# Carrying rows as fp16 halves out of attention: one DMA transpose for each x tile in place of TensorE transposes

## The reference

```python
h = tok(x)                                   # 768 -> 192, bias
h = layernorm(h + attn(h))                   # 12 heads of 16, tokens of one image
h = layernorm(h + ffn(h))
# ffn: y = expert(h, w1s, w2s, w3s)          (shared, width 768)
#      + sum over the best 2 of 8 experts of weight * expert(h, w1[e], w2[e], w3[e])
# expert(x) = (silu(min(x@W1, 10)) * clip(x@W3, -10, 10)) @ W2
# scores = sqrt(softplus(h @ gate_w)); choice by scores + gate_bias
```

## Time and profile before

| | us |
|---|---|
| median of 3 runs | 647.45 (644.85 to 650.32) |
| the profiled execution | 642.51 |
| its span, first to last instruction | 640.7 |
| PE busy | 540.3 |
| DVE busy | 455.9 |
| ACT busy | 357.5 |
| POOL busy | 182.8 |

### The profile page before, as it was taken

One profiled execution on the slowest core, in us unless ns is written; L12 is line 12 of the kernel. 1 busy time (PEld: TensorE's weight loads), 2 busy tenths in 40 slices (PEclk: granted clock), 3 DMA queues, 4 the chain that ended last, 5 costly groups with the idle time before them and its releaser, 6 DMA issues.

```text
span 640.7 us, 15246 instructions
## 1 busy us (share of the span) xinstructions
PE 540.3 (84%) x4208; PEld 410.0 (64%) x4209; DVE 455.9 (71%) x1064; ACT 357.5 (56%) x644; POOL 182.8 (29%) x210
## 2 busy tenths in 40 slices
PE   8899999899998668487739999999999999999451
PEld 7777878778787655275426666666666666667340
DVE  0376978878788766769836777777777777777385
ACT  1777696876968706544324555555555555555134
POOL 3102405224052221248750122221112222222422
PEclk9999999999999758989778999999999999999887
DMA  8334446364461513645534655555555555555833
GB/s 319 130 102 157 133 122 189 105 200 125 128 190 49 162 58 92 158 104 129 126 97 91 115 109 116 106 117 113 116 109 117 117 117 117 111 109 118 273 63 110
DMA packets 152890, 82.00 MB, mean 128 GB/s; under 512 B 120432, under 2 KB 148096, under 8 KB 151712
## 3 DMA queue, kind: packets, MB, share of 16 engines
q1 hardware_dynamic: 148144, 70.09, 45.1%
q0 software_dynamic: 4720, 11.60, 5.7%
HBM read 41.83 MB, written 15.83 MB: 90 GB/s over the span
## 4 chain that ended last, share of the span: by engine, by line
PE 64%; DVE 11%; POOL 8%; issue 8%; ACT 4%; DMA 4%; SPq 0%; ACTq 0%; DVEq 0%; POOLq 0%
PE bank L705 24%; PE bank L719 11%; PE bank L544 7%; POOL dbuf L1514 6%; DMA arena<-arena 3%; PE bank L622 3%; PE bank L571 3%; PE bank L583 3%; PE bank L693 3%; PE bank L634 3%; PE bank L559 3%; POOL rout L1477 1%; PE bank L637 1%; DVE arena L1015 1%; PE bank L742 1%
## 5 line engine op out<-in xcount | busy, mean ns | idle before, releaser
L705 PE MATMUL bank<-W,arena 128*128 (+1 forms) x1220 | 215.3, 333 | 2.1 <-DVE arena L1229 1.6
L705 PEld LDWEIGHTS bank<-W,arena 128*128 128x128 f16 x1220 | 120.5, 100 | 78.8 <-issue 7.7
L719 PE MATMUL bank<-W,arena 128*128 (+1 forms) x1098 | 102.7, 249 | 16.8 <-DVE arena L1238 16.8
L719 PEld LDWEIGHTS bank<-W,arena 128*128 128x128 f16 x1098 | 93.9, 99 | 25.7 <-issue 18.8
L1536 POOL DMA_INDIRECT ybuf<-arena,slot x43 | 41.9, 975 | 203.8 <-ACT arena L940 203.8
L1229 DVE TENSOR_SCALAR arena<-bank,sct 128x384 f32<-128x384 f32 x86 | 58.2, 677 | 39.9 <-PE bank L705 39.7
L924 ACT ACTIVATE arena<-bank,sct 128x384 f32<-128x384 f32 x86 | 49.9, 580 | 58.6 <-PE bank L705 58.5
L932 ACT ACTIVATE arena<-arena,sct 128x384 f16<-128x384 f32 x86 | 52.9, 615 | 46.3 <-DVE arena L1232 23.1
L1232 DVE SCALAR_TENSOR_TENSOR arena<-arena 128x384 f32<-128x384 f32 x122 | 68.3, 560 | 4.2
L1220 DVE SCALAR_TENSOR_TENSOR arena<-arena,sct 128x384 f16<-128x384 f32 x86 | 52.9, 615 | 15.8 <-ACT arena L932 15.7
L544 PE MATMUL bank<-arena,par 128*96 128x288 f32 x192 | 62.2, 416 | 0.5 <-ACT arena L832 0.5
(11 more groups left out here) (165 smaller groups left out, 836.6 us busy)
## 6 DMA issues: line engine op xcount, KB each, us to landing
arena<-xT SPq DMA_DIRECT2D x8, 864.0 KB, 4.7
stage<-w_all SPq DMA_DIRECT2D x9, 768.0 KB, 4.5
stage<-w_all SPq DMA_DIRECT2D x5, 1344.0 KB, 7.0
W<-w_all SPq DMA_DIRECT2D x4, 1344.0 KB, 7.1
arena<-dbuf SPq DMA_DIRECT2D x43, 96.0 KB, 2.0
dbuf<-arena SPq DMA_DIRECT2D x6, 679.0 KB, 9.1
W<-ybuf POOLq DMA_DIRECT2D x3, 1152.0 KB, 9.4
arena<-arena SPq DMA_TRANSPOSE x122
```

The costliest lines, as they stand in the source:

```text
L705: m = pe.matmul(bank[2 * k + n][:, 0:I // 2], xT16[:, b, lo, tail, :], W16[:, bass.ds(off + at + col, I // 2)], start=(z == 0), stop=(z == ...
L719: m = pe.matmul(bank[6][:, 0:C], hhT[b][:, ic // 3, lo, ic % 3, :], W16[:, bass.ds(off + at + ic * C, C)], start=(ic == 0 and z == 0), sto ...
```

## The change

A row is split once, in attention, and travels as fp16: 128 high values, 64 high values twice, 128 rest values, 64 rest values twice (HX = 512 numbers, 1024 bytes). A new DRAM buffer `xb16` holds these; `dbuf` rows grow from 194 to 264 fp32 words (the 512 halves, row number, weight, zeros). Each x tile is then one DMA transpose from `xb16` or `dbuf` straight into `xT16`: X, `x_hi`, `x_lo` and the three loads are gone (a load of 8 bytes a row stays for the routed steps). In attention POOL gets `split_rows(g)`, DVE `split_lo(g-1)`, SP `store_split(g-1)`. `hsp` has two buffers, so `h_hi(i)` waits for the transposes of step i-2 instead of i-1, and SP's `turn_h` stands after the x tile of two steps on (it was three). U(0) goes ahead of the last `proj`; the last `weights_lo_main` of attention goes behind `h_lo(0)`. COUNT_AT is 4, so the counts and choices are formed one step later. The core of the diff:

```diff
-HW = C + 2
+HX = 4 * C1
+DX = HX + 16
+HW = DX // 2
-            COUNT_AT = 3
+            COUNT_AT = 4
@@ SP, attention
+            def store_split(g):
+                sp.wait_ge(s_h16, g + 1)
+                sp.dma_start(xb16[bass.ds(g * GT, GT), :].rearrange("(t p) n -> p t n", p=TM),
+                             h16g).then_inc(s_x16o, 16)
@@ SP, group(g)
                 if choice:
                     zero_rows((g - 1) * ZPART, ZPART)
                     store_choice(g - 1)
+                if choice:
+                    store_split(g - 1)
                 if store:
                     store_group(g)
@@ POOL, attention
+            def split_rows(g):
+                wait_apart(pool, s_h1, g * GTILES + GTILES)
+                if not first(g):
+                    wait_apart(pool, s_x16o, g * 16)
+                PO.tensor_scalar(h16g[:, :, 0:C], h1g, XS, None, ALU.mult)
+                PO.tensor_scalar(h16g[:, :, C:2 * C1], h1g[:, :, C1:C], XS, None, ALU.mult).then_inc(s_h16h, 1)
...
                 if not last:
                     h0b_out(g + 1)
+                split_rows(g)
@@ DVE, attention
+            def split_lo(g):
+                wait_apart(dve, s_h16h, g + 1)
+                for at, a in ((2 * C1, 0), (2 * C1 + C, C1)):
+                    m = V.scalar_tensor_tensor(out=h16g[:, :, at:at + C - a], in0=h1g[:, :, a:C], scalar=XS,
+                                               in1=h16g[:, :, a:C], op0=ALU.mult, op1=ALU.subtract)
+                m.then_inc(s_h16, 1)
...
                 mask_max(g, 0)
                 weights_scale(g, wtotal)
+                if not start:
+                    split_lo(g - 1)
                 sums(g, 0)
                 mask_max(g, 1)
...
-                weights_lo_main(g, odd)
-                if last:
-                    x_lo(0, 0)
+                if not last:
+                    weights_lo_main(g, odd)
                 norm(g, between)
+                if last:
+                    split_lo(g)
                 between(ROUTE_G)
@@ SP, feed-forward
-            def load_x(row, b):
-                for at, a, n in ((0, 0, C1), (C1, C1, C2), (C, C1, C2)):
-                    sp.dma_start(xt[:, b, at:at + n], xbuf[bass.ds(row, XT), a:a + n]).then_inc(s_xl[b], 16)
+            def turn_x(n, b, rows):
+                if not (isinstance(n, int) and n < 2):
+                    wait_apart(sp, s_ud, n * 4 - 4)
+                sp.dma_start_transpose(xT16[:, b].rearrange("p z c n -> p (z c) n"), rows).then_inc(s_xl[b], 16)
...
                 def body(n, b):
-                    sp.wait_ge(s_xd, n - 1)
-                    load_x((n - skipped) * XT, b)
-                    turn_h(n - 3, 1 - b)
+                    turn_x(n, b, shared_rows(n - skipped))
+                    turn_h(n - 2, b)
@@ PE, feed-forward
             def U(i, b, off):
-                pe.wait_ge(s_xT, i + 1)
+                wait_apart(pe, s_xl[b], x_landed(i, b))
...
                 cur = cur(i)
-                if more:
-                    X(i + 1, 1 - b)
                 U(i, b, cur)
@@ ACT, feed-forward
-                    if not first(i):
-                        act.wait_ge(s_hT16[q], i * 16)
+                    if not (isinstance(i, int) and i < 2):
+                        act.wait_ge(s_hT16[b][q], (i - b) * 8)
```

More of the change, by code:

```diff
@@ L189, in over, with front @@
             return view(v.bitcast(F16) if dt == F16 else v, shape)
[L191 to L202, removed]
+        f_at = dict(zip([n for n, _ in F_SIZES], np.cumsum([0] + [n for _, n in F_SIZES]).tolist()))
+        def front(name, shape, dt=F32):
+            at = f_at[name]
+            v = arena[:, at:at + dict(F_SIZES)[name]]
+            return view(v.bitcast(F16) if dt == F16 else v, shape)
+        PSP = 1536
+        xT16 = front("xT16", (2, 2, 2, XT), F16)
+        sg, up = front("sg", (I,)), front("up", (I,))
+        hsp = [front("hsp0", (2, 2, I // 2), F16), view(par[:, PSP:PSP + I].bitcast(F16), (2, 2, I // 2))]
+        assert PSP + I <= PAR["wproj"][0]
+        yy = front("yy", (2, C))
+        hhT = [front(f"hhT{b}", (2, 2, IC // 2, XT), F16) for b in range(2)]
+        h16_raw = arena[:, H_FROM:H_FROM + SHT * HW]
+        h16 = view(h16_raw.bitcast(F16), (SHT, DX))
+        h16_id = view(h16_raw.bitcast(I32), (SHT, HW))[:, :, ROW_ID]
+        h16_w = view(h16_raw, (SHT, HW))[:, :, ROW_W]
+        h16_pad = view(h16_raw, (SHT, HW))[:, :, ROW_W + 1:HW]
+        h1 = acc = view(arena[:, H_FROM + SHT * HW:H_FROM + SHT * (HW + C)], (SHT, C))
+        assert H_FROM <= B_FROM
+        h16g = view(W16[0:TM, E * WF + 2 * (UPW + DNW):(E + 1) * WF], (GTILES, HX))
+        slot = view(slot_raw[:, :], (RTILES, 2))
         assert 2 * WF == SHT * 2 * C * 2
@@ L443, in _, with shared_rows @@
             group(GROUPS - 2, 0, load=False)
-            def load_x(row, b):
-                for at, a, n in ((0, 0, C1), (C1, C1, C2), (C, C1, C2)):
-                    sp.dma_start(xt[:, b, at:at + n], xbuf[bass.ds(row, XT), a:a + n]).then_inc(s_xl[b], 16)
[L450 to L473, removed]
+            def turn_x(n, b, rows):
+                if not (isinstance(n, int) and n < 2):
+                    wait_apart(sp, s_ud, n * 4 - 4)
+                sp.dma_start_transpose(xT16[:, b].rearrange("p z c n -> p (z c) n"), rows).then_inc(s_xl[b], 16)
+            def shared_rows(n):
+                return xb16[bass.ds(n * XT, XT), :]
             def turn_h(i, b):
@@ L517, in _ @@
             tiles_from(sp, SH2, ALLT, next_x(RTILES))
-            for i in range(ALLT - 3, ALLT):
+            for i in range(ALLT - 2, ALLT):
                 turn_h(i, i % 2)
@@ L772, in group @@
                 else:
[L773 to L774 removed]
+                    U(0, 0, 0)
                 proj(g)
@@ L796, in _ @@
             tiles_from(pe, SH2 + 2, ALLT - 1, lambda i, b: step(i, b, shared, shared))
-            step(ALLT - 1, (ALLT - 1) % 2, shared, shared, more=False)
+            step(ALLT - 1, (ALLT - 1) % 2, shared, shared)
             for i in (ALLT - 2, ALLT - 1):
@@ L949, in final_norm, with step @@
                 m.then_inc(s_fn, 1)
-            def step(i, b, cur, more=True):
-                if more:
-                    x_hi(i + 1, 1 - b)
+            def step(i, b, cur):
                 silu(i, scale(i, SILU_S) if cur else shc[:, SILU_S:SILU_S + 1])
-                h_hi(i, scale(i, H_S) if cur else shc[:, H_S:H_S + 1])
+                h_hi(i, b, scale(i, H_S) if cur else shc[:, H_S:H_S + 1])
             act.wait_ge(s_par, 32)
@@ L1241, in y_add, with step @@
                                        op0=ALU.mult, op1=ALU.add).then_inc(s_y, 1)
-            def step(i, b, cur, more=True, aside=None):
-                if more:
-                    x_lo(i + 1, 1 - b)
+            def step(i, b, cur, aside=None):
                 if aside:
@@ L1356, in _ @@
             up_h(0, *CLIPS)
-            x_lo(1, 1)
+            h_lo(0, 0, shc[:, H_S:H_S + 1])
+            weights_lo_main(GROUPS - 1, 1)
             steps = choice(GROUPS - 1)
@@ L1425, in _ @@
             for i in range(SH2, ALLT):
-                step(i, i % 2, False, more=(i < ALLT - 1))
+                step(i, i % 2, False)
                 if i > SH2 + 1:
```

154 lines of the change are left out of this document (83 added, 71 removed).

## The result

The kernel got slower. Against the kernel before, on one chip, the changed kernel takes 680.14 us (median of 4, 671.33 to 684.52) to 646.24 (median of 4). The forecast was 663 us, 639 to 681. On that chip the medians of the two kernels are 680.10 and 644.71.

The account below looks back on a forecast made before the run. PE was taken to set the pace in feed-forward, with DVE close beside it in attention. Attention +33.5, group 7 and start +8.5, first routed tile -3.5, steps 12 to 60 -18.5, end -4: +16 on 647.45, 663 us, range 639 to 681.

Parts of the forecast that it names:

- the first routed tile: From the last scatter to U(12): U(11) and D(9) done before, U(12) starting earlier but at the lower clock; -3.5 us.
- The wait: Attention: POOL's split waits for the previous group's store to land, holding DVE; 5.2 us a group after 1.42 us of slack.
- The clock: Attention: after idling, PE runs transposes and projections ahead of `heads` at the lower clock; 1.5 us a group (0 to 2.5).
- Steps 12 to 60: Routed steps: without X each step is 0.38 us shorter, the loop-end gap staying; -18.5 us.
- The sign that I had set down for being wrong: Profile signs against the forecast: landing under 4 us, POOL split under 1.2 us, or PE waiting for x tiles or h.
- rival (a): Routed steps: DMA transposes become the pace (SP or rings late), so the 18.5 us are not gained; +34, 682 us; 10%.
- Group 7 and start: Group 7's wait, U(0) ahead of `proj`, the added split and the later count, up to the first scatter; +8.5 us.
- The end: Last steps: two hsp buffers let h(58) split early, so D(57) follows the landing at once; -4 us.
- The point of decision: About 4.2 us a group in attention, above which attention costs more than feed-forward gives.
- rival (c): Attention: stores land before POOL asks, only DVE's hidden 1.15 us remain; -22, 625 us; 5%.

Follow-up runs that it names:

- e1: Changed kernel with SP issuing the store of the previous group's split rows ahead of its waits for the weights: 657.32 us, ratio 0.9805 to the kernel before.
- e6: Changed kernel with TensorE filling its 6.0 us attention wait with 26 unread products of ones: 664.60 us, ratio 1.0293 to the kernel before.
- e5: The changed kernel itself, run again on another chip: median 680.10 us beside 644.71 for the kernel before; profiled execution 675.86 us.
- e8: e1 with two unread fp32 transposes of the identity ahead of U from step 12 on: 634.96 us, ratio 0.9829 to the kernel before.
- e9: Changed kernel with early store, slot loads as one POOL DMA, and expert 1's weights at a fixed address in routed steps: 632.35 us, ratio 0.9435.
- e10: Changed kernel with early store, slot loads as one DMA, and TensorE's routed loop at four steps a turn, 6 offset loads for 8: 648.05 us, ratio 0.9672.
- e7: e1 with TensorE taking expert 1's weights at a fixed address in all routed steps: 629.36 us, ratio 0.974 to the kernel before.
- e4: Changed kernel with early store, slot loads as one DMA, and COUNT_AT back at 3: 660.14 us, ratio 0.9844 to the kernel before.
- e12: Kernel before with a second buffer for the split h and semaphores by buffer: 665.67 us, ratio 0.9946 to the kernel before.
- e11: Changed kernel with early store and slot loads as one POOL DMA, base run of the third group: 658.34 us, ratio 0.983 to the kernel before.

## Why the forecast came out as it did

The side was right and the time lies inside the range, at its upper end. The mechanism in attention is shown; one term of its size was off, and the largest gain of the sum did not come. That the time still fell into the range is partly luck: a gain that was counted and did not come (16 us) is made up in part by the first routed tile (5 us more than counted).

**The wait: right.** "The cost is in the order" is what e1 shows: nothing but the order was changed, and the period went from 34 to 37.5 back to 26.85. The steps on the way, counted from L429: forecast that `split_lo` ends at T0+10.3, measured 9.6 (163.49); store to landing forecast 6.1, measured about 5.5; POOL's split 2.2, measured 2.4; DVE's 1.15, measured 1.02. The 5.2 us for the wait are near the at most 4.8 of e6. (Two slips in the working have no weight: the split rows' 295 KB are in thousands of bytes beside 216 and 679 in 1024s, 288 on the page, and 48 x 0.38 is 18.2.) The rule of the Trainium skill (GPSIMD Engine Reference, Engine selection) that a one-input elementwise operation is roughly at line rate on GpSimd is not borne out: 1.65 and 0.69 us for 576 and 192 elements, fp32 to fp16, 2.3 times DVE's 1.02 us for its two operations on the same 768.

**The clock: the term that was mis-sized.** I put 1.5 us a group on it (0 to 2.5), counting only "about 3 us of transposes and projections ahead of `heads`" and hiding part of those behind ACT. e6 gives 2.6 in the groups of 34.2 us, just outside my bounds, and 5.9 in those of 37.5. In the latter PE stayed at the lower level through `heads` and the second projections, and these lie on the chain. In place of 6.7 us a group the first trace has 9.4 and e5's 8.0; over five groups that is 13 of the 24 us by which the sum was short in the first, and 6 of 17 in e5. I had the price of a U at the lower clock in the earlier trace rows, 2.4 to 2.6 us, and should have asked how much work at half speed follows an idle of 6 us, not only what stands right behind it. What decides between 34.2 and 37.5 stays open.

**Steps 12 to 60: the step that failed.** "Without X: 48 x 0.38 = -18.5 us" assumed two things; -2.6 came. First, that X's length in the chain of a routed step is its price. It is 0.21 us by the intervals of straight steps (4.95 and 4.74, and again 4.95 in e8), and the chain of the kernel before has it at 0.22 us there (587.26), which I didn't use. Second, that PE has nothing else on its own queue: "the rest being a gap at the loop's end that stays". The gap did not stay: over two straight steps a pair had 1.07 us more before and has 1.26 now. The offset loads need their time, X had covered a part of it, and without X the gap ahead of U grew, by the theory that e9 and e10 bear out. For SP I had 4.4 us a step. Its DMAs are 4.2 us a step, but registers and the like between them take about 1.2 more, where I had some 0.25: in the rows above the h transposes come again after 5.54 us and the slot load after 5.11, 10.7 a pair, and by e7 that alone holds the pair there. The sign that I had set down for being wrong came: PE waits for an x tile (0.79 us ahead of the U at 466.34). So rival (a), 682 us and 10%, named one of the two limits rightly; the measured 680 is close to it by a sum of other parts. U(12) at the lower clock costs 2.2 us of this stretch; without it the -2.6 would be -4.8, or 0.2 us a pair for 21 pairs.

**The first routed tile: right, too small.** I had the landing at 4.9 us after issue, from h's transposes, which go out two together; x's alone took 2.74. And I had charged U(12)'s lower clock to this term; it is real (5.46 us), but lies behind U(12)'s start. Together -6.2 for -3.5.

**Group 7 and start: +7.5 for +8.5;** the count is 1.1 of it or more (e4), the other parts of this term were not taken apart. **The end: -2.9 for -4,** by the one part to which I gave it (e12).

**The rivals.** The point of decision, 4.2 us a group, was passed by far. With attention repaired (e1) the change is worth 2%, some 13 us, not the 22 of rival (c), which is the same sum without the loss in attention.

## What to carry to other kernels

When a change gives a buffer a reader by DMA, look first where that DMA stands in its queue: the same store, issued 2 us after its rows were ready in place of 28, turned 7 to 11 us of loss a group into none. Before pricing a removed instruction at its length in the chain, look what its own queue does meanwhile (loads of registers, loop turns) and take the interval between its neighbours where it is missing; and relieve all queues of a like pace in one experiment, since here one at a time showed nothing. An idle TensorE costs more than the idle: price the work behind it at the lower clock as far as it reaches.

## What the runs showed of the hardware beyond what I had expected

- After an idle of 6.04 us PE's matmuls ran at the lower clock for 12.1 us (165.80 to 177.90, granted 0.50), and in a group of 34.2, after an idle of 6.34 us, for 5.4 us (203.66 to 209.05, granted 0.51), though it was busy all the while (12.08 and 5.39 us); filling the idle with 6.02 us of products kept the granted clock of the stretch at 1.00, and gained 10 to 15.5 us in all.
- On two of the three chips of the experiments, TensorE issues its matmuls one by one while POOL scatters, at distances that are near multiples of 0.7 us. Timeline of e11, and the stretch of the scatters in e12 and, on another chip, in the kernel before (columns as in the earlier trace rows):

```profile
301.37 0.48 PE L723 MATMUL bank<-W,arena 128*128 128x384 f16 x1 [1.62 <-issue]
302.10 0.48 PE L723 MATMUL bank<-W,arena 128*128 128x384 f16 x1 [0.25 <-issue]
303.50 0.48 PE L723 MATMUL bank<-W,arena 128*128 128x384 f16 x1 [0.93 <-issue]
306.30 0.48 PE L723 MATMUL bank<-W,arena 128*128 128x384 f16 x1 [2.32 <-issue]
```

```profile
281.00:329.00 48.00, 17.21 (x93) 8.62 (x91) 10.14 (x27) 8.94 (x11) 35.43 (x40) 0.62 0.32 92
```

```profile
281.00:329.00 48.00, 34.63 (x255) 23.55 (x252) 37.69 (x78) 19.49 (x33) 37.93 (x38) 0.91 0.55 132
```

  PE gets through 93 matmuls where it does 255 elsewhere; DVE and ACT starve as well (27 and 11 for 78 and 33), the scatters themselves go on. U(12) then waits for the shared steps, and the kernel before takes 22.5 to 25.2 us more on these chips (668.76 and 669.88 to 646.24 and 644.71). What in the scatters does this, and why not on every chip, no run here tests.
- A DMA transpose of a 128x512 fp16 tile from DRAM costs SP 1.19 us of its queue, as much as one of h from SBUF (1.22), and landed 2.6 us after issue at the least and 3.2 in the median of 43.
